# A one-core metaformer kernel: the filling reordered, and centring ahead of the output sum

## The reference, cut to what matters

```python
x = x + conv(ln_c(x))            # block 1
t = tokens(x); t = t + ffn(ln_t(t))   # block 2

# ln_c, ln_t: (v - mean) / sqrt(var + eps) over the 48 channels of a pixel
# conv: a 3x3 convolution on the first 12 channels; 1x1 to 254 channels;
#       per 8x8 patch: rfft2, times fft_w, irfft2; gelu(first half) * second half;
#       1x1 back to 48 channels
# ffn:  inputs and weights rounded to a float of 5 exponent and 2 mantissa bits,
#       48 -> 192, relu, 192 -> 48, sums rounded to float16
```

## Time and profile before

| | us |
|---|---|
| median of 3 runs | 819.62 (816.13 to 821.55) |
| profiled execution | 817.74 |
| its span | 815.9 |

### The profile page before, as it was taken

The page is one execution under the profiler, slowest core; times in us unless marked ns, Lnnn a source line. Parts: engine busy times, 40 slices in busy tenths (PEclk is TensorE's granted clock), DMA queues, the critical chain, the costliest instruction groups (busy, mean ns, idle before and its releaser), DMA issues.

```text
span 815.9 us, 20717 instructions
## 1 busy us (share of the span) xinstructions
PE 715.8 (88%) x6571; PEld 526.6 (65%) x6571; DVE 626.7 (77%) x1157; ACT 507.7 (62%) x962; POOL 575.8 (71%) x420
## 2 busy tenths in 40 slices
PE   1318999999998999989998999989999999999963
PEld 0207776767677676767776677767777767677731
DVE  5515788888887888878887888878888888877761
ACT  2114366767676666666776676766776766666674
POOL 2534768888777678788777778878788777854362
PEclk9999999999999999999999999999999999999995
DMA  3123333333333233333333133323333323232001
GB/s 64 43 65 71 75 69 94 94 89 78 82 93 89 59 82 93 94 93 65 92 89 91 52 89 93 94 77 80 91 92 89 81 68 87 75 89 55 20 20 39
DMA packets 46497, 62.38 MB, mean 76 GB/s; under 512 B 19039, under 2 KB 34871, under 8 KB 46391
## 3 DMA queue, kind: packets, MB, share of 16 engines
q1 hardware_dynamic: 46391, 61.00, 29.9%
HBM read 44.62 MB, written 16.35 MB: 75 GB/s over the span
## 4 chain that ended last, share of the span: by engine, by line
PE 80%; DVE 7%; issue 5%; ACT 2%; POOL 2%; DMA 1%; DVEq 0%; POOLq 0%; SPq 0%; ACTq 0%
PE mixp L436 15%; PE inva L449 14%; PE invb L454 14%; PE misc L535 8%; PE misc L463 8%; PE misc L497 5%; PE misc L482 3%; DVE gmix L807 3%; PE misc L592 3%; PE misc L491 2%; PE misc L551 2%; PE misc L523 2%; PE misc L554 2%; ACT xpix L675 2%; POOL st L978 1%
## 5 line engine op out<-in xcount | busy, mean ns | idle before, releaser
L807 DVE TENSOR_TENSOR gmix<-mixp,freq_w 128x508 f32<-128x508 f32 x256 | 163.9, 682 | 55.4 <-PE mixp L436 52.0
L644 ACT ACTIVATE hid<-misc 128x512 f16<-128x512 f32 x192 | 100.9, 598 | 82.3 <-PE misc L497 82.3
L449 PE MATMUL inva<-inv,gmix 128*127 128x128 f32 x1024 | 135.0, 274 | 0.9 <-DVE gmix L807 0.9
L449 PEld LDWEIGHTS inva<-inv,gmix 128*127 128x127 f32 x1024 | 128.3, 191 | 11.4 <-issue 2.0
L454 PE MATMUL invb<-inv,gmix 128*127 128x128 f32 x1024 | 134.4, 274 | 0.0
L436 PE MATMUL mixp<-win,zh 60*128 60x254 f16 x1024 | 119.8, 271 | 16.0 <-DVE gmix L807 14.6
L454 PEld LDWEIGHTS invb<-inv,gmix 128*127 128x127 f32 x1024 | 123.8, 191 | 0.0
L436 PE MATMUL mixp<-win,zl 60*128 60x254 f16 x1024 | 118.6, 267 | 0.0
L653 ACT ACTIVATE hid<-hid 128x512 fp8e5<-128x512 f16 x192 | 106.2, 627 | 0.0
L970 POOL TENSOR_TENSOR ob<-tch,y 112x1024 f32<-112x1024 f32 x32 | 68.3, 2135 | 51.2 <-DVE y L881 51.2
L1013 POOL TENSOR_TENSOR st<-st,neg_half 128x16 f32<-128x16 f32 x32 | 92.9, 2903 | 10.8 <-DVE st L927 10.8
(11 more groups left out here) (103 smaller groups left out, 1261.7 us busy)
## 6 DMA issues: line engine op xcount, KB each, us to landing
xin<-in_x_dram SPq DMA_DIRECT2D x64, 192.0 KB, 3.5
xres<-in_x_dram SPq DMA_DIRECT2D x64, 192.0 KB, 3.9
out_dram<-ob SPq DMA_DIRECT2D x64, 192.0 KB, 3.2
taps<-cz_scratch SPq DMA_DIRECT2D x32, 292.5 KB
crm<-rm_scratch SPq DMA_DIRECT2D x64, 96.0 KB
cz_scratch<-cz SPq DMA_DIRECT2D x64, 48.8 KB
cx<-in_x_dram SPq DMA_DIRECT2D x32, 96.0 KB
rm_scratch<-rm_t SPq DMA_DIRECT2D x128, 4.0 KB
```

Of the source, the lines that this page charges most:

```text
L449: mm = pe.matmul(inva[0:HID, q * PX:(q + 1) * PX], gmix[:, s % 2, q, 0:HID], inv[:], start=True, stop=True, skip_group_check=True)
L644: act.activation(hid16[:, 3 * c + g, :], bank[banks[g]][:], ACT.Copy).then_inc(hid16_ready, 1)
L807: dve.tensor_tensor(gmix[:, s % 2, 2 * q:2 * q + 2, 0:HID2], mixp[q][:, 0:2 * HID2].rearrange("p (e c) -> p e c", e=2), freq_w[:], ALU.mul ...
```

## The change

On SP, x of step 1 is issued ahead of the constants, and a row-out of the statistics is split from its row-in for the first two steps, ahead of loads and stores; the biases move behind the first row-out and have a semaphore of their own. The four zero-row transfers are issued by ScalarE before its first activation, and are waited for at the first load of `taps`. DVE clears `zero_row` and `xin` first, and each half of `xin` is announced by itself. PE, ScalarE and DVE take the row statistics of the first steps in other places. On POOL, the convolved channels of turn 2 come in the order of the full steps (right behind `xsq`), and in every step `xcen` is computed ahead of the output sum and of the power, where it stood behind both.

```diff
@@ SP
             sp.wait_ge(x_zeroed, 1)
             load_x((0, 0), 0)
             load_cx((0, 0), 0)
-
+            sp.wait_ge(x_zeroed, 2)
+            load_x((0, 0), -1)
             sp.dma_start(raw_fft[:], fft_w.rearrange("(g p) a b u v -> p g (a b u v)", g=2)).then_inc(const_in, 16)
...
+            def biases():
+                with nc.allow_non_contiguous_dma(reason="small weights, once"):
+                    sp.dma_start(raw_b[:, 0:1], b1[0:128].rearrange("(p o) -> p o", o=1)).then_inc(bias_in, 16)
+                    for j in range(2):
...
-                for part in range(2):
-                    for r in (0, PR - 1):
...
-                        sp.dma_start(images[:, :, r, :], zero_row[0:CC, :].unsqueeze(1).to_broadcast([CC, BATCH, PW]))\
-                          .then_inc(pads_out, 16)
-                sp.wait_ge(pads_out, 16 * 4)
+            def rows_out(t):
+                a = at(t, 0)
+                sp.wait_ge(rmT_ready, upto(a + 1))
+                for kind in range(2):
+                    for j in range(2):
+                        q = (kind * 2 + j) * PAIRS
+                        dst = rm_d[ring(t, 0), kind, j * PATCH:(j + 1) * PATCH]
+                        sp.dma_start(dst.rearrange("r (i w) -> i r w", w=TW),
+                                     rm_t[q:q + PAIRS, :].rearrange("i (r w) -> i r w", w=TW))\
+                          .then_inc(rm_out, 16)
+
+            def rows_in(t):
+                a = at(t, 0)
+                sp.wait_ge(rm_out, upto(64 * (a + 1)))
+                sp.wait_ge(csub, upto(a))
+                sp.sem_inc(sp_held, 1)
+                for kind in range(2):
+                    src = rm_d[ring(t, 0), kind].rearrange("(g q) w -> g (q w)", g=CG)
+                    sp.dma_start(crm[:, kind, :], src.unsqueeze(0).to_broadcast([CC, CG, 2 * W]))\
+                      .then_inc(rm_in, 16)
...
             def step(t):
+                early = isinstance(t[0], int) and t[1] < 2
-                if live(t, -1):
+                if live(t, -1) and not (isinstance(t[0], int) and t[1] == 0):
...
                     load_x(t, -1)
                 if live(t, 3):
...
                     load_res(t, 3)
+                if early:
+                    if a == 0:
+                        setup()
+                    rows_out(t)
+                    if a == 0:
+                        biases()
                 if live(t, 0) and not (isinstance(a, int) and a == 0):
...
                     load_cx(t, 0)
+                if early:
+                    rows_in(t)
                 if live(t, 1):
...
                 if live(t, 2):
                     c = at(t, 2)
+                    if isinstance(c, int) and c == 0:
+                        sp.wait_ge(pads_out, 16 * 4)
...
-                if isinstance(t[0], int) and t[1] == 0:
-                    setup()
-                if live(t, 0):
+                if live(t, 0) and not early:
+                    rows_out(t)
+                    rows_in(t)
@@ PE
-                pe.wait_ge(const_in, 16 * (9 + 6 + 5))
+                pe.wait_ge(const_in, 16 * (9 + 6))
...
+            def rows(t, behind):
+                a, n, m = (at(t, d) for d in (behind, 3, 4))
+                pe.wait_ge(mr_ready, upto(a + 1))
+                pe.wait_ge(mr_half, upto(a + 1))
+                if isinstance(t[0], int):
+                    pe.wait_ge(lo_ready, upto(2 * n + 2))
+                pe.wait_ge(rmT_ready, upto(a))
+                pe.wait_ge(tpix_ready, upto(2 * m + 2))
+                pe.transpose(bank[3][0:32, 0:128], rm[:].rearrange("p a j i -> p (a j i)"), eye[:])\
+                  .then_inc(rmT_done, 1)
...
-                    pe.wait_ge(rmT_ready, upto(before(0)))
+                    pe.wait_ge(rmT_ready, upto(before(0) if t[1] > 1 else 0))
...
+                    if peeled and a == 1:
+                        rows(t, 1)
...
-                if live(t, 0):
...
+                if live(t, 0) and not (peeled and a == 0):
+                    rows(t, 0)
@@ ScalarE
+            act.wait_ge(row_zeroed, 1)
+            for part in range(2):
+                for r in (0, PR - 1):
+                    images = cz_d[part].rearrange("c (b r) w -> c b r w", b=BATCH)
+                    act.dma_start(images[:, :, r, :], zero_row[0:CC, :].unsqueeze(1).to_broadcast([CC, BATCH, PW]))\
+                      .then_inc(pads_out, 16)
             order_x((0, 0), 0)
...
+                filling = isinstance(t[0], int) and t[1] < 3
...
+                if filling and t[1] == 1:
+                    rows(t, 1)
+                if filling and t[1] > 0:
+                    rows(t, 0)
                 if live(t, -1):
                     order_x(t, -1)
...
-                if live(t, 0):
+                if live(t, 0) and not filling:
+                    rows(t, 0)
@@ DVE
+            dve.memset(zero_row[:], 0.0).then_inc(row_zeroed, 1)
+            for half in range(2):
+                dve.memset(xin[:, half, :], 0.0).then_inc(x_zeroed, 1)
             dve.memset(neg_half[:], -0.5).then_inc(set_dve, 1)
             dve.memset(rm[:], 0.0).then_inc(set_dve, 1)
-            dve.memset(xin[:, 0, :], 0.0).then_inc(set_dve, 1)
-            dve.memset(xin[:, 1, :], 0.0).then_inc(set_dve, 1)
...
-                dve.tensor_copy(b8[:], raw_b[:], saturate=False).then_inc(set_dve, 1)
...
+                dve.wait_ge(bias_in, 16 * 5)
+                dve.tensor_copy(b8[:], raw_b[:], saturate=False).then_inc(set_dve, 1)
...
+                if isinstance(a, int) and a == 1:
+                    rows(t, 1)
...
-                if live(t, 0):
+                if live(t, 0) and not (isinstance(a, int) and a == 0):
+                    rows(t, 0)
@@ POOL
                 pool.wait_ge(rm_in, upto(32 * (z + 1)))
+                pool.wait_ge(cz_ready, upto(z))
                 pool.tensor_tensor(cz[:], cx[:], crm[:, 0], ALU.mult).then_inc(cmul, 1)
...
-                filling = isinstance(t[0], int) and t[1] < 3
+                filling = isinstance(t[0], int) and t[1] < 2
...
                 if not filling and live(t, 1):
                     convolved_channels(t)
+                if live(t, 0):
+                    st1 = st1s[:, ring(t, 0)]
+                    pool.wait_ge(mean1, upto(a + 1))
+                    pool.wait_ge(zpix_ready, upto(a - 1))
+                    mean = st1[:, 2, :].unsqueeze(2).to_broadcast([128, 2 * PAIRS, REST])
+                    pool.tensor_tensor(xcen[:, ring(t, 0)], halves(xpix)[:, :, CC:CH], mean, ALU.subtract)\
+                        .then_inc(xcen_ready, 1)
                 if live(t, 6):
...
                 if live(t, 0):
-                    st1 = st1s[:, ring(t, 0)]
                     pool.wait_ge(zpix_ready, upto(a - 1))
                     pool.wait_ge(stat1, upto(4 * a + 4))
                     pool.tensor_tensor(st1[:, 6, :], st1[:, 5, :], neg_half[:], ALU.pow).then_inc(pow1, 1)
...
                 if filling and live(t, 1):
                     convolved_channels(t)
-                if live(t, 0):
-                    pool.wait_ge(mean1, upto(a + 1))
-                    pool.wait_ge(zpix_ready, upto(a - 1))
-                    mean = st1[:, 2, :].unsqueeze(2).to_broadcast([128, 2 * PAIRS, REST])
-                    pool.tensor_tensor(xcen[:, ring(t, 0)], halves(xpix)[:, :, CC:CH], mean, ALU.subtract)\
-                        .then_inc(xcen_ready, 1)
```

More of the change, by code:

```diff
@@ L158, in metaformer_kernel @@
         const_in = sem("const_in")
+        bias_in = sem("bias_in")
         x_in = [sem(f"x_in{p}") for p in range(2)]
@@ L194, in metaformer_kernel @@
         y16_ready = sem("y16_ready")
+        row_zeroed = sem("row_zeroed")
         x_zeroed = sem("x_zeroed")
+        small_set = sem("small_set")
         zeroed = sem("zeroed")
@@ L344, in setup @@
-                sp.wait_ge(pads_out, 16 * 4)
+                                     b2.rearrange("(p o) -> p o", o=1)).then_inc(bias_in, 16)
+            def rows_out(t):
[8 more added lines that the diff above has]
+                          .then_inc(rm_out, 16)
@@ L654, in activations, with rows @@
                        .then_inc(hid8_ready, 1)
+            def rows(t, behind):
+                a = at(t, behind)
+                act.wait_ge(rmT_done, upto(a + 1))
+                act.wait_ge(rm_out, upto(64 * a))
+                act.activation(rm_t[:], bank[3][0:32, 0:128], ACT.Copy).then_inc(rmT_ready, 1)
             def order_x(t, behind):
@@ L745, in _ @@
         def _(dve):
+            dve.memset(zero_row[:], 0.0).then_inc(row_zeroed, 1)
+            for half in range(2):
+                dve.memset(xin[:, half, :], 0.0).then_inc(x_zeroed, 1)
             dve.memset(neg_half[:], -0.5).then_inc(set_dve, 1)
             dve.memset(rm[:], 0.0).then_inc(set_dve, 1)
-            dve.memset(xin[:, 0, :], 0.0).then_inc(set_dve, 1)
-            dve.memset(xin[:, 1, :], 0.0).then_inc(set_dve, 1)
-            dve.wait_ge(set_dve, 4)
```

(25 more changed lines are left out.)

14 lines of the change are left out of this document (4 added, 10 removed).

## The result

| | before | changed |
|---|---|---|
| median of 4 runs | 820.59 | 832.0 |
| range | 816.13 to 822.75 | 829.51 to 834.3 |
| profiled execution | 817.74 | 831.13 |
| its span | 815.9 | 829.3 |

The ratio is 1.0146 (1.0092 to 1.0199): slower by 1.5%. The forecast was slower by 0.7%, 823.7 us, with a range of 809 to 831; the measured median lies 1.0 above that range.

A forecast was written before the change was run, and what follows sets the result against it. PE was taken to bound the kernel once its pipeline is full, with time won or lost only where PE waits. 817.74 less 13.9 for the filling plus 19.9 for the collision gave 823.7 us, range 809 to 831.

The forecast's parts named there:

- Part 1: The filling: earlier SP issues and convolved work right behind xsq start step 3 at 47.5 instead of 61.36, gaining 13.9 us.
- The same chain of issues: SP's issues from its first to the end of raw_pc, assumed to take 15.94 us as before, so raw_pc ends at 18.0.
- rival C: In the head, ScalarE's zero-row issues hold up SP's by 3.46 us, giving 827.2 with the collision; chance 0.13.
- (a): In the filling, DVE's weight preparation, 31.99 to 40.73 before, would be done before the tap matmuls near 43.4.
- (b): Step 2's power, now behind convolved work and xcen, finishes its row near 41.8, with 1.8 us of room before tap matmuls.
- (c): Step 1's row-out needs that step's power; copied out about 23.6, wanted by SP at 24.8: 1 us of room.
- Part 2: Every step: xcen ahead of the output sum blocks DVE's two-SBUF-operand statistics, delaying PE's second mix 0.8 us; 19.9 us lost.
- two cases in the price: xcen delays DVE's first small statistic by 1.05 us, or slips in behind it and delays the second by 0.9; 0.95 taken.
- 23 full turns: Of steps 3 to 31, 23 were expected to lose the full 0.8 us each to the collision, 18.4 in all.
- six exceptions: Steps 3, 4, 12, 16, 20 and 24, expected to escape the collision wholly or in part, adding 1.5 us together.
- A: No collision: POOL picks xcen up after DVE's 0.14 us window and waits itself; 803.8, up to 808; chance 0.13.
- B: Mixed case: DVE shifts and part of the steps escape, half the collision loss; 813.8, between 808 and 818; chance 0.12.

The follow-up runs named there:

- experiment 9: Kernel of 1, with ScalarE's four zero-row transfers moved from the start to turn 1, behind the first row copy; one run, 809.76 us.
- 2: Kernel before the change, with only xcen moved ahead of the output sum in all turns; ratio 1.0298 to the kernel before.
- 1: Changed kernel with xcen put back behind the power from turn 3 on, new filling kept; ratio 0.9859 to the kernel before.
- 3: Changed kernel with xcen between the output sum and the power from turn 3 on; ratio 0.9899 to the kernel before.
- 4: Changed kernel with xcen's subtract replaced by a POOL memset of the same tile from turn 3 on; ratio 0.9857 to the kernel before.
- 5: Changed kernel with 14 extra PE transposes in turns 3 and 4, and qpix's eight transposes done twice in later turns; ratio 1.03 to the kernel before.
- 6: Changed kernel with 14 extra PE transposes ahead of the second mix in turns 3 and 4 only; ratio 1.01 to the kernel before.
- 7: Kernel of 1 plus both PE additions of 5 (14 extra transposes, qpix transposes doubled); ratio 1.0201 to the kernel before.
- 8: Kernel of 7 with the hardware loop as one iteration of 20 turns instead of five of four; ratio 0.984 to the kernel before.
- 10: Kernel of 1 plus 14 extra PE transposes in turns 3 and 4 and one loop iteration of 20 turns; ratio 0.97, median 795.65 us.
- 11: Changed kernel with only the loop made one iteration of 20 turns; ratio 1.0041 to the kernel before.

## Why the prediction missed

- **Part 1, mechanism right, 1.0 us too high.** Every foreseen time came about 1 us late from raw_pc on (18.80 for 18.0, 24.99 for 24.0, 37.05 for 36.1, 48.47 for 47.5). The step at fault: "The same chain of issues takes 19.12 - 3.18 = 15.94". It took 16.76 in its new order. Zero rows on ScalarE, rival C's place, cost SP some tenths at most (experiment 9), not 3.46.
- **What could be late next.** (a), (b) and (c) all held: rows of step 2 were at SP by 42.12, and the tap matmuls did not wait for them (their row transpose was at 41.42, they started at 44.42). The room that the prediction gives (b), 1.8, is 1.6 by its own numbers (43.4 less 41.8).
- **Part 2, the collision.** Right, shown four times: made by the move alone (2), undone by taking it back (1), gone with another neighbour on DVE (3) or with a memset in place of the subtract (4). Of the two cases in the price, it is the dearer: L874's successor is caught, and it loses 1.04. The count of 23 full turns was right, and the six exceptions were those foreseen. The term was 19.9 and measured 21.2: 0.87 a turn, not 0.8.
- **The step that failed is the sum.** "817.74 - 13.9 + 19.9" has no term for PE's granted clock. Three more stretches at half clock than in the kernel before were 5.1 (4.8 by the lengths of turns) of the 7.4 us by which the profiled 831.13 lies above 823.7; the head makes 1.0, the collision 1.3. The range, too, had no room for it: its upper end by its own terms, 817.74 - 11 + 23 + 1.9, would have been 831.6, and it was stated as 831. The trace before had shown what it would have taken: two stretches of half clock in turns 12 and 20, and PE idle for 1.5 and 1.44 us ahead of the second mix in turns 3 and 4, which the collision lengthened to 2.25 and 1.77.
- **How far the clock is shown.** That idle PE is needed for it is well supported: in turns 3 to 5 the clock fell in six of the eight profiles without added PE work, and in none of the five with it (5, 6, 7, 8, 10); from turn 6 to the end of the full turns it fell only behind a border of the loop, and never in 8, 10 and 11, which have none. That longer waits made it fall is not shown, and some rows speak against it. The waits of 1.50 and 1.44 us in turns 3 and 4 stand unchanged in the kernel before, 1, 4 and 9: no fall in the kernel before and in 4, one in turn 3 of 1, and a stretch of twice the length in 9. In 9 and 11 the clock fell 1.0 and 1.4 us before the wait ahead of the second mix was over, so its end played no part. It is partly chance, and what decides it stays open. The five runs of 10 lie within 1.3 us and have one mean clock (0.984 to 0.985); 15 runs of the kernel before spread from 816.87 (clock 0.984) to 823.42 (clock 0.975).
- **Rivals.** A and B did not come, beyond the six exceptions that the sum already had: 0.14 us decided, and POOL took xcen up without a gap. C's time was the nearest to what came, by a cause that was not there: SP's first issue was at 2.04, and the constants followed it without a long gap while ScalarE sent its rows.

The Trainium skill says of this (TensorE: Matmul & The Clock Gate, HAM oscillation — how this bites in real kernels) that in one kernel waits for DMA between bursts of matmuls bring the array back to half clock each time. The trace agrees that half clock comes with waits: 0.50 granted for 3.4 us after PE had idled for 2.25. But waits of 1.4 to 2.3 us, between stretches of full work, are followed by a fall in one profile here and by none in another.

## What to carry to other kernels

An engine's idle gap is free room only if nothing that runs beside it on another engine is held up: before a GpSimd instruction is moved, list the DVE instructions at its new place that have two operands in SBUF, and whether DVE has slack there. Here 1.15 us of POOL work put in a 0.88 us gap cost 0.87 us in each turn; one place further on it cost nothing. And when a change lengthens or shifts PE's waits, read the granted clock by microsecond before and after: each fall costs about 1.6 us here, and in the five kernels with added matmuls in the wait none came there.

## What the runs showed that I had not expected

- A border of the hardware loop stopped PE, DVE and ScalarE, and POOL once its power was done. In the five kernels with full turns of 22.4 us and a body of four turns (before, 1, 3, 4, 9), a turn with a border took 24.3 to 24.9 us where the clock stayed up and 25.9 to 26.2 where it fell behind the border. With eight more matmuls a turn in the body it took 28.8 to 30.9. What the engines wait for there, no row shows. One iteration of 20 turns took it away, about 10 us in all here (experiment 1's four turns with a border took 10.5 more than four full ones).
- Fourteen transposes in PE's waiting time (1.75 us) cost about 0.1 us at most (turn 3 took 18.58 in experiment 7 and 18.47 in 4), and the clock stayed up.
- A POOL memset beside a DVE instruction with two SBUF operands does not hold it up (0.16 us); a subtract that writes the same tile does (1.2 us).
